# Two residual convolutions: small weights issued by ScalarE, band loads held back in TensorE's first full step, last steps run inside the loop, another finish of the last half image

## The reference

```python
def _gn(v, G=16, eps=1e-05):
    g = v.reshape(B_, G, C_ // G, H_, W_)
    m = jnp.mean(g, axis=(2, 3, 4), keepdims=True)
    s = jnp.var(g, axis=(2, 3, 4), keepdims=True)
    return ((g - m) / jnp.sqrt(s + eps)).reshape(v.shape)

x = x + _L0_conv_ref(_gn(x), L0_conv_weight, L0_conv_threshold)   # 3x3, weights masked by a threshold
x = x + _L1_conv_ref(_gn(x), L1_conv_kernel, L1_conv_bias)        # 5x5 (written with an FFT), plus a bias
return x
```

## Time and profile before

| | us |
|---|---|
| median of 3 runs | 831.24 (830.08 to 831.35) |
| the profiled execution, its own time | 827.96 |
| its span, first to last instruction | 826.1 |
| TensorE busy | 755.1 (91% of the span) |
| VectorE busy | 608.1 (74%) |
| ScalarE busy | 335.5 (41%) |
| GpSimd busy | 259.8 (31%) |

### The profile page before, as it was taken

One profiled execution on the slowest core, in us unless ns is written; L12 is line 12 of the kernel. 1 busy time (PEld: TensorE's weight loads), 2 busy tenths in 40 slices (PEclk: granted clock), 3 DMA queues, 4 the chain that ended last, 5 costly groups with the idle time before them and its releaser, 6 DMA issues.

```text
span 826.1 us, 67771 instructions
## 1 busy us (share of the span) xinstructions
PE 755.1 (91%) x32292; PEld 535.1 (65%) x32292; DVE 608.1 (74%) x970; ACT 335.5 (41%) x291; POOL 259.8 (31%) x162
## 2 busy tenths in 40 slices
PE   0786499999999999999999999999999999998795
PEld 0344277777786766766776766777766777665463
DVE  5897569787878798797878787887978785745241
ACT  0351226353444436363534444363634353443410
POOL 1040033222333343432223343333222333333221
PEclk9998689999999999999999999999999999999998
DMA  8999978898998979798989979797987676753224
GB/s 170 191 205 220 223 170 189 196 223 196 217 216 194 214 171 223 182 219 202 225 199 214 217 185 223 168 223 184 223 196 177 137 177 151 167 122 75 58 51 102
DMA packets 234118, 150.59 MB, mean 182 GB/s; under 512 B 18592, under 2 KB 227552, under 8 KB 229984
## 3 DMA queue, kind: packets, MB, share of 16 engines
q1 hardware_dynamic: 228768, 144.67, 79.6%
q10 hardware_dynamic: 4608, 4.23, 2.2%
q0 software_dynamic: 704, 1.25, 0.6%
HBM read 75.60 MB, written 33.59 MB: 132 GB/s over the span
## 4 chain that ended last, share of the span: by engine, by line
PE 88%; DVE 4%; issue 3%; DMA 1%; SPq 1%; ACT 1%; DVEq 0%; ACTq 0%; POOLq 0%; POOL 0%
PE psum L836 66%; PE psum L854 21%; DMA x_bands<-x_dram 1%; DVE x_lo L695 1%; DVE bn_in L591 1%; DVE mid L715 1%; DVE bn_out L723 0%; DVEq L718 0%; SPq L255 0%; SPq L279 0%; ACT conv_out L453 0%; ACTq L487 0%; ACT x_hi L384 0%; POOLq L58 0%; DVE x_bands L667 0%
## 5 line engine op out<-in xcount | busy, mean ns | idle before, releaser
L358 POOL TENSOR_TENSOR mid<-mid,conv_out 128x512 f32<-128x512 f32 x122 | 246.9, 2056 | 513.8 <-ACT conv_out L453 513.8
L836 PE MATMUL psum<-x_hi,s_hi 32*64 32x512 f16 x6656 | 200.5, 382 | 16.0 <-ACTq L487 6.2
L836 PE MATMUL psum<-x_lo,s_hi 32*64 32x512 f16 x6656 | 199.0, 381 | 4.1 <-DVE x_lo L695 3.8
L836 PE MATMUL psum<-x_hi,s_lo 32*64 32x512 f16 x6656 | 197.4, 377 | 0.0
L836 PEld LDWEIGHTS psum<-x_hi,s_hi 32*64 32x64 f16 x6656 | 124.9, 105 | 80.2 <-issue 10.0
L836 PEld LDWEIGHTS psum<-x_hi,s_lo 32*64 32x64 f16 x6656 | 136.9, 104 | 47.5 <-issue 1.0
L836 PEld LDWEIGHTS psum<-x_lo,s_hi 32*64 32x64 f16 x6656 | 109.0, 104 | 80.3 <-issue 10.6
L715 DVE SCALAR_TENSOR_TENSOR mid<-psum,unscale,x_own 128x1024 f32<-128x1024 f32 x64 | 79.2, 1279 | 105.3 <-PE psum L854 105.3
L453 ACT ACTIVATE conv_out<-psum,bias,unscale 128x512 f32<-128x512 f32 x122 | 85.2, 777 | 83.9 <-PE psum L836 83.9
L377 ACT ACTIVATE x_hi<-x_bands 128x2304 f16<-128x2304 f32 x31 | 65.6, 2117 | 115.3 <-PE psum L854 115.2
L703 DVE TENSOR_TENSOR x_lo<-mid_bands,x_hi 128x2560 f16<-128x2560 f32 x32 | 91.7, 2864 | 11.0 <-PE psum L836 10.8
(11 more groups left out here) (89 smaller groups left out, 333.0 us busy)
## 6 DMA issues: line engine op xcount, KB each, us to landing
x_own<-x_dram SPq DMA_DIRECT2D x128, 256.0 KB, 5.0
mid_bands<-mid SPq DMA_DIRECT2D x372, 80.0 KB, 2.7
out_dram<-mid SPq DMA_DIRECT2D x116, 256.0 KB, 5.2
x_bands<-x_dram SPq DMA_DIRECT2D x96, 288.0 KB, 6.0
x_bands<-x_dram SPq DMA_DIRECT2D x32, 272.0 KB, 5.9
mid_bands<-mid SPq DMA_DIRECT2D x124, 64.0 KB, 2.6
every_mv<-mv_scratch ACTq DMA_DIRECT2D x16, 256.0 KB, 4.1
out_dram<-mid SPq DMA_DIRECT2D x24, 128.0 KB, 2.4
```

The lines of the kernel that those rows point to most:

```text
L358: nc.gpsimd.tensor_tensor(m, m, conv_out[:, b, :], ALU.add).then_inc(out_added, 1)
L836: ins = nc.tensor.matmul(psum[2 * C * J:2 * C * (J + 1), bank + i, :].rearrange("p (a w) -> p a w", a=A), w[quad(i), at:at + 2, :].rearran ...
```

## The change

There are five edits. (a) The 3x3 weights, the threshold and the mixing matrix `mix_in` are issued by ScalarE's queue rather than by SyncE's. (b) In TensorE's first full step (step 3), the loads of bands 6, 7, 8 and of `x_own` 4 are held back until the semaphore `a5_whole` tells that step's high parts of the 5x5 are done; from then on band loads run one half image less ahead. Because bands 6 and 7 come later, their statistics (image 3) are taken in step 4 and get an exchange of their own there, and `normalize3(6)` comes behind it (`just_now`). VectorE's work in step 3 is put in another order, and `largest(w5, 1)` moves to a later place. (c) TensorE's last steps are no copy any more: `whole_step` is cut into labelled parts, and the last three steps run `conv5` and `conv5_rest` of the loop and skip the rest. (d) For the last half GpSimd adds the bias to `mid` ahead of time, and VectorE finishes each pair of banks with one operation. (e) The stores of the last half are issued by SyncE and ScalarE, half each.

```diff
@@ SyncE @@
-            for q in range(Q):
-                sp.dma_start(w3[quad(q), :, :], w3_dram.rearrange("i a b o -> i (a b) o")).then_inc(w3_loaded, 16)
-            sp.dma_start(thr[:, :], thr_dram.rearrange("(a o) -> a o", a=1).to_broadcast([P, 1])).then_inc(w3_loaded, 16)
             load_bands(0)
             load_bands(1)
-            sp.dma_start(mix_in[:, :], mix_dram).then_inc(mix_loaded, 16)
             load_bands(2)
...
             load_bands(5)
             move_mid(2)
+            sp.wait_ge(a5_whole, 1)
+            load_own(LAG + 1)
+            move_edges(1, 1, 0)
             load_bands(6)
             load_bands(7)
-            load_own(4)
+            move_edges(1, 0, 1)
+            move_mid(LAG)
+            load_own(LAG + 2)
             load_bands(8)
 
-            for s in range(LAG, STEPS + 1):
+            for s in range(LAG + 1, STEPS + 1):
...
-                if has3(s + XB_SLOTS):
-                    sp.wait_ge(norm1, s + 2)
-                    load_bands(s + XB_SLOTS)
+                if has3(s + XB_SLOTS - 1):
+                    sp.wait_ge(norm1, s + 1)
+                    load_bands(s + XB_SLOTS - 1)
@@ ScalarE @@
+            for q in range(Q):
+                act.dma_start(w3[quad(q), :, :], w3_dram.rearrange("i a b o -> i (a b) o")).then_inc(w3_loaded, 16)
+            act.dma_start(thr[:, :], thr_dram.rearrange("(a o) -> a o", a=1).to_broadcast([P, 1])).then_inc(w3_loaded, 16)
+            act.dma_start(mix_in[:, :], mix_dram).then_inc(mix_loaded, 16)
...
+            for g, banks in enumerate(LAST_GROUPS):
+                act.wait_ge(last_out, g + 1)
+                for j in range(Q // 2, Q):
+                    act.dma_start(own_rows(out[LAST // 2], LAST % 2, j)[:, A * banks.start:A * banks.stop, :],
+                                  as_rows(mid, j, LAST % MID_SLOTS, banks)).then_inc(out_stored[LAST % MID_SLOTS], 16)
@@ GpSimd @@
+                if k == LATE:
+                    pool.wait_ge(norm2, HALVES)
+                    m = mid[:, LAST % MID_SLOTS, :, :]
+                    nc.gpsimd.tensor_scalar(m, m, bias[:, 0:1], None, ALU.add).then_inc(bias_added, 1)
@@ VectorE @@
-            dve.wait_ge(w_loaded, 16 * 2 * Q)
-            largest(w5, 1)
             take_conv3(0)
...
             low3(2)
+            dve.wait_ge(w_loaded, 16 * 2 * Q)
+            largest(w5, 1)
...
-            take_conv3(LAG)
-            stats_out(LAG)
             dve.wait_ge(mv_in, 16)
             group_stats(("x", 2))
             scale_of(("x", 2))
             normalize3(LAG + 1)
-            stats_in(6, range(BANKS))
-            stats_in(7, range(BANKS))
-            aggregate("mid", LAG // 2)
-            aggregate("x", (LAG + 3) // 2, mv_ready)
+            take_conv3(LAG)
+            stats_out(LAG)
+            aggregate("mid", LAG // 2, mv_ready)
             low3(LAG + 1)
...
-            take_late(HALVES - 1)
-            add_late(HALVES - 1)
+            dve.wait_ge(b5_whole, LAST + 1)
+            dve.wait_ge(bias_added, 1)
+            for at in LAST_GROUPS:
+                m = mid[:, LAST % MID_SLOTS, at, :]
+                nc.vector.scalar_tensor_tensor(m, psum[:, X5_BANK + at.start:X5_BANK + at.stop, :], unscale[:, 1:2], m,
+                                               ALU.mult, ALU.add).then_inc(last_out, 1)
@@ TensorE @@
+            with nc.body("conv5", valid_engines=only):
                 pairs5_high()
+                pe.br_lt(step, HALVES, on_true="conv3_rest", on_false="conv5_rest")
+            with nc.body("conv3_rest", valid_engines=only):
                 singles3()
+            with nc.body("conv5_rest", valid_engines=only):
                 singles5()
-                pairs5_low(step)
-                pe.br_lt(step, HALVES, on_true="whole_step", on_false="before_last").branch_hint(hint)
-            with nc.body("before_last", valid_engines=only):
-                pe.br("last_steps")
+                pe.reg_add(step, step, 1)
+                pairs5_low()
+                pe.br_lt(step, HALVES, on_true="whole_step", on_false="last_steps").branch_hint(hint)
             with nc.body("last_steps", valid_engines=only):
-                pairs5_high()
-                singles5()
-                pairs5_low(step)
-                pe.br_lt(step, STEPS, on_true="last_steps", on_false="all_done")
+                pe.br_lt(step, STEPS, on_true="conv5", on_false="all_done")
```

More of the change, by code:

```diff
@@ L63, in sem @@
             return ctx.enter_context(nc.semaphore(name))
-        mv_dram = nc.dram_tensor("mv_scratch", (N, P, 2, 2), F32, kind="Internal").ap()
+        mv_dram = nc.dram_tensor("mv_scratch", (N + 1, P, 2, 2), F32, kind="Internal").ap()
         x_bands = sbuf("x_bands", [P, XB_SLOTS, R3, W])
@@ L176, in two_blocks @@
         late_added = sem("late_added")
+        bias_added = sem("bias_added")
+        last_out = sem("last_out")
         def has3(s):
@@ L184, in exchanged @@
         def exchanged(s):
-            if s == 2:
-                return [("x", 2)]
-            if not (3 <= s < HALVES and s % 2):
+            if s in (2, LAG + 1):
+                return [("x", 2 if s == 2 else LAG)]
+            if not (LAG <= s < HALVES and s % 2):
                 return []
-            return [("mid", s // 2)] + ([("x", (s + 3) // 2)] if (s + 3) // 2 < N else [])
+            return [("mid", s // 2)] + ([("x", (s + 3) // 2)] if LAG < s and (s + 3) // 2 < N else [])
+        EXCHANGES = [s for s in range(HALVES) if exchanged(s)]
         def exchange_number(s):
-            return 1 if s == 2 else s // 2 + 1
+            return EXCHANGES.index(s) + 1
         LATE = HALVES - LAG
         HALF_BANKS = BANKS // 2
+        LAST = HALVES - 1
+        LAST_GROUPS = (slice(HALF_BANKS, BANKS), slice(0, HALF_BANKS))
         def added_before(k, b):
@@ L245, in load_own, with store_out @@
                                  ).then_inc(x_own_in[h % X_SLOTS], 16)
-            def store_out(k, banks):
-                for j in range(Q):
+            def store_out(k, banks, quads=range(Q)):
+                for j in quads:
                     sp.dma_start(own_rows(out[k // 2], k % 2, j)[:, A * banks.start:A * banks.stop, :],
@@ L310, in _ @@
                         store_out(k, slice(0, BANKS))
+                    elif k == LAST:
+                        for g, banks in enumerate(LAST_GROUPS):
+                            sp.wait_ge(last_out, g + 1)
+                            store_out(k, banks, range(Q // 2))
                     else:
@@ L358, in add_out @@
                 nc.gpsimd.tensor_tensor(m, m, conv_out[:, b, :], ALU.add).then_inc(out_added, 1)
-            for k in range(HALVES):
+            for k in range(LAST):
                 for b in range(BANKS if k < LATE else HALF_BANKS):
                     add_out(k, b)
+                if k == LATE:
+                    pool.wait_ge(norm2, HALVES)
+                    m = mid[:, LAST % MID_SLOTS, :, :]
+                    nc.gpsimd.tensor_scalar(m, m, bias[:, 0:1], None, ALU.add).then_inc(bias_added, 1)
         @block.scalar
@@ L477, in _ @@
                 gathered = exchanged(s - 1)
-                if has5(s - 1):
+                if has5(s - 1) and s <= LAST + LAG:
                     k = s - 1 - LAG
@@ L481, in _ @@
                         take_conv5(k, b)
-                if s > HALVES:
+                if HALVES < s <= LAST + LAG:
                     act.wait_ge(late_out, s - HALVES)
@@ L799, in _ @@
                     add_late(s - 1 - LAG)
-                if has3(s + 1):
+                just_now = ("x", (s + 1) // 2) in gathered
+                if has3(s + 1) and not just_now:
                     normalize3(s + 1)
@@ L807, in _ @@
                     scale_of(stat)
+                if just_now:
+                    normalize3(s + 1)
                 if s % 2:
@@ L814, in _ @@
                     stats_out(s)
-                if exchanged(s):
+                if s == LAG + 1:
+                    for h in (2 * LAG, 2 * LAG + 1):
+                        stats_in(h, range(BANKS))
+                    aggregate("x", LAG, mv_ready)
+                elif exchanged(s):
                     aggregate("mid", s // 2, None if len(exchanged(s)) > 1 else mv_ready)
@@ L889, in singles5, with pairs5_low @@
                 singles(s5_lo, x5_hi, K5, X5_BANK).then_inc(a5_whole, 1)
-            def pairs5_low(step):
-                pe.reg_add(step, step, 1)
+            def pairs5_low():
                 pairs(s5_hi, x5_lo, K5, X5_BANK, every=x5_lo_go).then_inc(b5_whole, 1)
```

## The result

The changed kernel takes 823.73 us (median of 5 runs, 823.08 to 826.0), the kernel before 831.24 (5 runs, 829.8 to 832.0): a ratio of 0.993, interval 0.9908 to 0.9952. By the medians 7.5 us are won (by the ratio 5.8), less than half of the 15.4 that the sum had. The profiled execution took 823.28, with a span of 821.5.

A forecast was written before the change was run, and what follows sets the result against it. TensorE was taken as busy throughout whole steps, so gains lay only in the start, step 3, step 32 and the tail. The terms summed to -15.4 us, 831.24 becoming 815.8, range 807 to 825.

The forecast's parts named there:

- the start: Before step 3: bands issued earlier win 2.1 us (between -2.9 and -0.5); moving largest(w5, 1) costs 0.7.
- steps 4 to 6: Holding loads back makes TensorE wait for VectorE in steps 5 and 6: +5.6 us, between +2.6 and +11.
- the last steps: Steps 32 to 34, run in the loop's code without instruction fetches: -4.9 us, between -4.9 and -7.0.
- the branch: The new branch in the loop, taken 29 times, mostly covered by queued matmuls: +1.0 us, between 0 and 2.6.
- tail: After TensorE ends, VectorE's first operation lets two queues start storing sooner: -1.9 us, between -1 and -2.5.
- step 3: TensorE's first full step: with bulk loads held back, code fetches stall it less, -13.8 us.
- The 2.9 to be won: At the start: band 1 issued 3.2 us earlier lands as much earlier, winning 2.9 if the weights land as before.
- rival A: VectorE's exchanges set steps 3 to 6, gathers staying slow: -9 and +11, sum -5.2, 826 us; chance 0.18.
- rival B: Held loads do not speed the fetch, so step 3 wins nothing: -1.6, 829.6 us; chance 0.07.
- Rival C: The new branch breaks TensorE's run; over 0.57 us lost per step makes the change lose; chance 0.05.
- Rival D: Jumps into the middle of the loop refetch code: last three steps +9.8 instead of -4.9, 830.5 us; chance 0.04.
- The 2.0 "which stays": Step 32: 2.0 us of slow matmuls behind a 2.96 wait for ScalarE were expected to remain.

The follow-up runs named there:

- bands_wait: The changed kernel, but SyncE issues no band before the weights on ScalarE's queue have landed; 823.05 us (a single run).
- exchange_quiet: The changed kernel with weights' loads back on SyncE, statistics of bands 6 and 7 early in step 4, band 8 onward held until image 3's gather landed; 818.68 us.
- stats67_early: The changed kernel, but VectorE takes the statistics of bands 6 and 7 ahead of the 3x3 result in step 4; 821.02 us.
- hold89: The changed kernel with edits (a) and (b) undone, and only x_own 4, band 8 and what follows held until a5_whole of step 3; 820.1 us.
- combined2: As combined, but in step 5 VectorE makes low3(6) before the statistics of bands 8 and 9, and ScalarE sends that step's exchange one step later; 815.33 us.
- b_undone: The changed kernel with the loads, exchanges and VectorE's order of step 3 as before, except the later largest(w5, 1); 826.95 us.
- pad24: The changed kernel with edit (a) undone and 24 further instructions behind the new branch, 2051 in the loop; 1320.03 us (a single run).
- c_alone: The kernel before with edit (c) alone: the last three steps run inside the loop's code; 822.52 us.
- pad16: The changed kernel with edit (a) undone and 16 further instructions behind the new branch, 2043 in the loop; 867.62 us (a single run).
- a_undone: The changed kernel with the loads of weights, threshold and mixing matrix back on SyncE's queue; 817.5 us.
- combined: The changed kernel with edit (a) undone, statistics of bands 6 and 7 early in step 4, and largest(w5, 1) at its old place; 815.32 us.

## Why the prediction was right or wrong

The sign was right, and the size was less than half of what was forecast. In the profiles -15.4 became -4.6, 10.8 off: 7.4 at the start, 6.5 in steps 4 to 6, against 2.0 and 0.6 too little credited to the last steps and to the branch, and 0.4 and 0.1 to tail and step 3.

**The start: the step that failed.** "They now share the engines with the bands ... so I put them 0.8 later", bounds -2.9 to -0.5. The weights and the threshold let VectorE begin 8.35 later than before, and with `largest` the stretch measured +6.0 instead of -1.4. The row leaned on, 9.2 us for 256 KB in step 3, already showed a transfer that lands late among its neighbours; I read it as a matter of its size ("these are smaller"). The three starts 6.34, 10.21 and 14.94 show that it is not: half a kilobyte is late by what is queued beside it. When the threshold was issued, four band transfers had been (1.2 MB); when it landed, SyncE's queue had moved 2.68 of the twelve's 3.5 MB. So it waited for more than the bulk issued ahead of it. The Trainium skill's page DMA: Bandwidth & Descriptors (section Queues, rings and completion order) has a rule that fits: a completion's semaphore write from a DMA engine lands only behind every earlier write of that engine, across its queues. The landings just before 10.21 and 14.94 agree with it; no run here tells it from other forms of waiting behind the bulk.

I had only asked how the engines' bandwidth is shared. The 2.9 to be won "if the weights land as before" is shown by no run either: in `bands_wait`, with the bands issued 2.3 later than before, band 1's statistics start 0.4 earlier. So the term's step from an earlier issue to an equally earlier landing of band 1 has no support.

**Steps 4 to 6: right mechanism, half the size, the second step that failed.** The term was +5.6 and measured +12.1. The wait came where it was forecast, at the 3x3 lows of step 5 (3.64 for 2.6), and slow matmuls behind it. The granted clock was 0.50 from 134.90 to 137.50, and the 48 and 160 matmuls there took 2.79 and 5.99. The 1.0 more has its own cause: the gather of step 4, issued at 108.76, landed only at 118.90, so that VectorE took the 3x3 result at 122.16, T + 16.7 instead of T + 15.4. Then, +5.6 took the exchange of image 3 at 2.4 + 3.6 and it measured 15.7, so step 6 waited twice more. This was rival A's "+11 for 5 and 6", which I had joined to a slow exchange in step 3. The two are not one event: in step 3 the exchange was quick (3.3 and 3.4) and the -13.8 came (-13.7 from the first singles on), and the +11 came too.

`exchange_quiet` shows why the gather is slow. The other runs show that the cost moves rather than goes: `stats67_early` has it at step 6, `hold89` already at the start of step 5, `exchange_quiet` at step 6 through bands 8 and 9, `combined2` at step 7. The reading, argued and not shown by a run of its own, is that the 4.7 MB of bands 6 to 9 and what was queued with them must cross in steps 4 and 5, where the exchange must cross as well.

What remains open is which order of these loads is the best; four were tried.

**Step 3, the code and the last steps: right.** `b_undone` shows the stalls shrinking with the traffic (rival B, dead: with the loads back, 5.44, 3.99, 5.32 and 3.56). That the stalls are code being fetched rests on the packets and on `pad24`, where packets and stalls appear together. The size of step 3's term came out nearly exactly, but one part otherwise than written: the singles waited 1.44 and 1.74 as forecast (1.6), while the last 160 pairs did not wait for code and took 6.1 instead of 4.4, at a granted clock of 0.72.

Rival C is dead: 22.81 per step with the branch, and `c_alone` lost nothing by it, so +1.0 should have been none. The Trainium skill's page Advanced Engine Details and Errata (section Control Flow Timing), with its 108 ns a branch, would add 3.1. No part of that is to be seen here, where the branch stands behind queued matmuls. Rival D is dead: one packet in the last steps and no stall. The Trainium skill's page Runtime: NRT & Kernel Launch (section Instruction fetch mechanics) has the rule that only two blocks of 16 KB are held. It is spoken against again by `pad16`, eight blocks long and free of packets. The same section of the Trainium skill also gives TensorE's memory as 2048 instructions, and with that number `pad16` and `pad24` agree.

**The 2.0 "which stays" did not.** Behind the wait of 2.96 at step 32 the 160 matmuls took 4.61 in the changed kernel. In other kernels whose code there is the same, behind waits of 2.94 to 2.96, they took 4.60 (`a_undone`, `b_undone`), 5.93 (`combined`), 6.24 (`hold89`) and 7.48 (`bands_wait`). Each kernel has one profile, so whether this scatters from run to run or is fixed by each kernel's timing stays open. The 2.0 of the last steps beyond the forecast were thus luck, and the term should have been a range.

**Tail:** -2.3 for -1.9. TensorE ends at 813.9, the first store goes out at 815.28, and GpSimd's bias pass (6.41 for 128x2048, at 782.64) was hidden.

Of the signs named ahead, those of step 3, of the loop and of step 5's wait (3.64 for 2.6) came, and one instruction packet was left in the last steps where none was named. The second statistics near 17.5, step 4 near 98, "hardly one" wait in step 6 and the first store near 804 did not.

## What to carry to other kernels

Issue a small load that starts a chain ahead of the bulk; another queue did not protect it here. With 12 bulk transfers beside it, 0.5 KB let its reader start at 14.9 us instead of 6.3. Holding loads back from a stage where code is fetched for the first time paid here (16.5 us), but ask in which stage they go instead, and what short exchange must pass them there (12.1 given back). Price a repeated exchange at its slow landing wherever the edit itself adds traffic beside it. Run each part of an edit alone: one of the five won as much as all five together.

## What was not expected of the hardware

- 24 added instructions turned a loop of 22.8 us into one of 39.9, 16 added ones into 24.6: the edge lies between 2043 and 2051 instructions, and eight instructions cost 15.3 us a step.
- Sixteen instructions that only raise a semaphore opened a gap of 1.72 us, 107 ns each, while a branch in the same place cost nothing that 29 steps show.
- A write of 2 KB took 7.7 us and a gather of 256 KB 8.0, at 237 and 214 GB/s on the transfer engines; in step 3 of the same kernel, at 53 and 81 GB/s, they took 3.3 and 3.4.
- After nearly the same wait of about 2.95 us, 160 equal matmuls took from 4.60 to 7.48 us in the profiles of different kernels.
